# Row maxima of an attention kernel: turned on VectorE by 32x32 blocks instead of on TensorE, with four transfers per half

## The chip, the cores and the metric

The kernel runs on one core of a Trainium2 chip. The metric is the device time of one execution in microseconds (us), the median of several executions. PE is TensorE's matmul, PEld its weight load, DVE is VectorE, ACT is ScalarE, POOL is GpSimd, SP is SyncE, which here only issues transfers.

## What is computed

```python
def proj(W):                                   # x: 8 x 512 x 1024 (batch, channel, token)
    y = jnp.einsum('oc,bct->bto', W, x)
    return y.reshape(B, T, H, Dh).transpose(0, 2, 1, 3)      # 16 heads of 32
Q, K, V = (proj(Wq), proj(Wk), proj(Wv))
att = jnp.einsum('bhqd,bhkd->bhqk', Q, K) * (1.0 / math.sqrt(Dh)) + b[0]
att = att * m + (1.0 - m) * NEG_INF            # m: mask over the keys
att = jax.nn.softmax(att, axis=-1)
y = jnp.einsum('bhqk,bhkd->bhqd', att, V).transpose(0, 2, 1, 3).reshape(B, T, C).transpose(0, 2, 1)
# then, for every row y[b, c, :] of 1024:
q, in_scale = per_token_quant_int8(y)          # absmax / 127, round, clip
out = x + float16(einsum('bsk,nk->bsn', q, weight) * in_scale * w_scale + bias)
```

## The kernel before, in words

The kernel has two parts. `project` computes Q, K and V of all 8 batches, splits Q and K each into a high and a low float32r part and writes them to memory (0 to about 555 us of the span). `attend` runs 32 **steps**; step s is four heads of one batch (`STEPS = B * G`), and all the rest of this section is about it.

**A step has 64 slots** (`UNITS`), t = 0 to 63: two halves of the queries (512 each), times 8 tiles of 128 keys, times 4 heads. In slot t TensorE makes one score tile of 128 keys x 512 queries (L798, in one of three PSUM banks) and ScalarE takes its exponential into `probs` (L932). Since keys lie on the partitions, the row maximum that softmax subtracts can't be a bias of that exponential. It is put into the product instead: `q_stack` has, below the rows of Q, two rows (`ROW_MAX`, partitions 98 and 99) with the high and the low part of minus the row maximum of every query, and `k_stack` has ones there.

**The row maxima are made one step ahead.** In slot t TensorE also makes one tile of 128 queries x 512 keys (L147, `row_max`) into a ring of four PSUM banks, and VectorE reduces it (L154, `reduce_max`). 64 such tiles belong to a step, two for each of 32 pairs (head, tile of queries). The pairs are in two chunks of 16, one per half of the queries. Slots 20 to 63 of step s and slots 0 to 19 of step s+1 make the maxima of step s+1. Chunk 0 of step s+1 is complete at slot 51 of step s, and its rows are needed by slot 0 of step s+1. Chunk 1 of step s is complete at slot 19 of step s and needed by slot 32 (L794: `pe.wait_ge(max_rows[half], ...)`).

**From maxima to rows**, for each chunk: VectorE joins the two halves of a pair, twice over, into 128 x 32 (`join_max`, L161, at slots 19 and 51). TensorE transposes that against an identity into a ring bank (`turn_max`, L169, at slots 20 and 52, `TURN_1` and `TURN_0`). ScalarE takes the high parts (`high_max`, L176) and VectorE the low parts (`low_max`, L182), with a per-partition mark that tells high rows from low rows. SP writes the two rows with one transfer of 32 x 128 elements (`store_max`, L189), whose semaphore `max_rows` TensorE waits for.

**Order of work.** Each engine has its own program, written out by hand slot by slot; only semaphores tie them. What matters here:

- TensorE (`step` of `block.tensor`): in each slot the score, then the row-max tile. After slots 3, 11, 19, 27, 35, 43, 51 and 59 it makes a burst of 16 products probs x V (L829, `weigh`). After slot 27 it also makes the row sums of the step before (L839), after slot 55 eight transposes of the quantised rows (L862), after slot 59 the row sums and the 16 matmuls of the feed-forward product (L872). Each tile that takes a ring bank waits until the bank's last user is done; the list `USES` gives the order, in which each row-max tile, `turn`, `sums` and so on takes the next of the four banks.
- ScalarE: one exponential per slot, and between them copies. Some rows of the next step's `k_stack` and `q_stack` are copies of other rows (`double_k`, L963, two after slot 19 and two after slot 27; `double_q2`, L973, after slots 35 and 59; L968 after slot 59). `take_y` (L937) after slots 3 and 35 empties the bank of the probs x V product. `round_rows` follows slot 43, `make_ints` slot 51. At slot 35 `take_y` comes first, then `double_q2`.
- VectorE: one reduction per slot; `take_absmax` of half 0 and `take_floor` after slot 19 (L1042, L1047), `recip` after slots 27 and 59 (L1028, L1031), `spread` after slots 3 and 31 (L1037), `take_absmax` of half 1 and `scales` after slot 39, `take_qT` at 55.
- GpSimd: additions of whole tiles of exponentials (L1177, `acc`, 128 x 2048, both inputs in SBUF), accumulating transfers (L1161), normalisation (L1184), bias and residual (L1190, L1198), in one fixed order per step. Its transfer for tile pair 2 of half 1 (`begin_pair(s, 1, 2)`) waits for the burst after slot 59, the one for pair 2 of half 0 for the burst after slot 27.
- SP: in each step the transfers of K, of the output, `store_max` for chunk 1, then the loads of Q's second half (`load_q`, L117) and of V, and at the end `store_max` for chunk 0.

Of the kernel before, what the change touches and what calls it, by code (L numbers as in the profile page):

```python
# [25 lines left out]
P = 128  # L26
# [43 lines left out]
EXTRAS = {TURN_1: ("turn",), SUMS_1: ("sums",), TURN_0: ("turn",), TURN_Q: ("turn_q",),  # L70
# [6 lines left out]
MAX_ROWS = 16  # L77
# [80 lines left out]
def join_max(nc, dve, half_max, neg_max, s, chunk, neg_max_done, joined):  # L158

    dve.wait_ge(neg_max_done, HALVES * s + 2 * CHUNK * (chunk + 1))  # L160
    nc.vector.tensor_reduce(neg_max[:, chunk, :].rearrange("p (d c) -> p d c", d=2),  # L161
                            half_max[:, chunk, :, :].rearrange("p (o c) k -> p o c k", o=1).to_broadcast([P, 2, CHUNK, 2]),
                            AX_X, ALU.min).then_inc(joined, 1)


def turn_max(pe, buf, neg_max, ident, s, chunk, joined, maxT_done):

    pe.wait_ge(joined, 2 * s + chunk + 1)
    pe.transpose(buf[0:2 * CHUNK, 0:P], neg_max[:, chunk, :], ident[:, :]).then_inc(maxT_done, 1)  # L169


def high_max(nc, act, buf, max_parts, marks, s, chunk, maxT_done, max_rows, max_hi_done):

    act.wait_ge(maxT_done, 2 * s + chunk + 1)
    wait(act, max_rows[chunk], MAX_ROWS * s)
    nc.scalar.activation(max_parts[:, chunk, :], buf[0:2 * CHUNK, 0:P], ACT.Identity, scale=marks[:, 1:2]).then_inc(max_hi_done, 1)  # L176


def low_max(nc, dve, buf, max_parts, marks, s, chunk, max_hi_done, max_lo_done):

    dve.wait_ge(max_hi_done, 2 * s + chunk + 1)
    nc.vector.scalar_tensor_tensor(max_parts[:, chunk, :], buf[0:2 * CHUNK, 0:P], marks[:, 0:1],  # L182
                                   max_parts[:, chunk, :].bitcast(F32), ALU.mult, ALU.subtract).then_inc(max_lo_done, 1)


def store_max(sp, q_stack, max_parts, par, chunk, max_rows):

    dst = q_stack[par][ROW_MAX:ROW_MAX + 2, chunk, :, :]
    sp.dma_start(dst.bitcast(F32), max_parts[:, chunk, :].bitcast(F32)).then_inc(max_rows[chunk], 16)  # L189


def project(nc, x, mask, wqT, wkT, wvT, qk_d, v_d, bias_d, cond_b, fw, wT, ws_rep, fb_rep, w_scale, f_bias,
# [6 lines left out]
    with ExitStack() as ctx:  # L199
# [54 lines left out]
        def _(sp):  # L254
# [22 lines left out]
            def batch(b, par, last=False):  # L277
# [10 lines left out]
                for tt in range(TT):  # L288
                    if last and tt == TURN_STORE:
                        sp.wait_ge(max_lo_done, 1)  # L290
                        store_max(sp, q_stack, max_parts, 0, 0, max_rows)
# [1011 lines left out]
```

## Time and profile before

| | us |
|---|---|
| median of 3 runs (2295.03 to 2297.74) | 2297.32 |
| the profiled execution, its own time | 2295.35 |
| its span in the trace | 2293.5 |
| PE busy in the span (98%) | 2249.3 |
| POOL busy (74%; 272.4 of the 300 us from 900 to 1200) | 1708.3 |
| DVE busy (70%; 260.4 of the same 300 us) | 1616.1 |
| ACT busy (67%; 243.6 of the same 300 us) | 1538.4 |

The projection fills the first quarter of the span, where VectorE, ScalarE and GpSimd have little to do; the rest is the 32 steps, in which every engine is busy most of the time. Matmul records overlap, so the busy time of PE is not its load: the chain of waits, which gives each piece the time that it adds, is the better view of TensorE. The granted clock of TensorE is 1.00 of full (2.4 GHz) throughout.

### The profile page before, as it was taken

Reading aid. Unit: us, or ns where it says so; the run is one execution under the profiler, and the core shown is the slowest. Engines: PE = TensorE matmul, PEld = TensorE weight load, DVE = VectorE, ACT = ScalarE, POOL = GpSimd, SP = SyncE. Lnnn points to the kernel's source line nnn. Section 1 sums busy time; section 2 is a strip of 40 time slices with the busy share of each in tenths; the row PEclk is TensorE's granted clock in tenths of the full one; section 3 lists DMA queues with packets and bytes.
Section 4 is the critical chain, followed back from the end, with each engine's and each line's share of the span. In section 5 each row is a group of like instructions: output and inputs, shape, how many; then the busy total and the mean of one; then the engine's idle time right before and its main releaser. Section 6 shows DMA issues by size and latency. Waiting matters only on the chain.

```text
span 2293.5 us, 34614 instructions
## 1 busy us (share of the span) xinstructions
PE 2249.3 (98%) x11892; PEld 1354.8 (59%) x11924; DVE 1616.1 (70%) x2779; ACT 1538.4 (67%) x2681; POOL 1708.3 (74%) x735
## 2 busy tenths in 40 slices
PE   9999999999999999999999999999999999999998
PEld 7888888887555555555555555555555555555553
DVE  3311111117888888888888888888888888888883
ACT  3322222223788888887887888888888887888774
POOL 2322333322899998989999998998989989998996
PEclk9999999999999999999999999999999999999999
DMA  6665545575888888888888888888888888888874
GB/s 238 253 229 193 183 183 215 189 219 145 188 186 188 185 185 189 185 191 189 194 187 189 178 189 183 190 187 187 187 184 187 189 188 191 189 189 189 181 155 109
DMA packets 137909, 433.27 MB, mean 189 GB/s; under 512 B 12248, under 2 KB 48088, under 8 KB 113440
## 3 DMA queue, kind: packets, MB, share of 16 engines
q0 software_dynamic: 27360, 199.24, 44.2%
q1 hardware_dynamic: 101040, 205.85, 29.5%
q10 hardware_dynamic: 9360, 26.22, 3.2%
q8 instruction: 91, 1.49, 0.3%
q14 instruction: 58, 0.48, 0.1%
HBM read 130.06 MB, written 100.93 MB: 101 GB/s over the span
## 4 chain that ended last, share of the span: by engine, by line
PE 91%; ACT 3%; POOL 2%; DMA 2%; issue 1%; DVE 0%; POOLq 0%; ACTq 0%
PE score L798 21%; PE pv L829 20%; PE ring L147 19%; PE ring L344 11%; PE score L344 9%; PE ring L872 4%; PE pv L344 3%; PE ring L839 2%; POOL acc L1177 2%; DMA probs<-probs 1%; ACT q_stack L973 1%; ACT probs L932 1%; PE ring L862 1%; ACT y_raw L937 1%; PE ring L169 0%
## 5 line engine op out<-in xcount | busy, mean ns | idle before, releaser
L154 DVE TENSOR_REDUCE half_max<-ring 128x1 f32<-128x512 f32 x2048 | 1261.9, 678 | 92.2 <-PE ring L147 84.4
L932 ACT ACTIVATE probs<-score 128x512 f32<-128x512 f32 x2039 | 1032.6, 615 | 235.0 <-PE score L798 233.5
L1177 POOL TENSOR_TENSOR acc<-acc,probs 128x2048 f32<-128x2048 f32 x189 | 903.6, 4781 | 29.0 <-DMA probs<-probs 26.9
L798 PE MATMUL score<-q_stack,k_stack 100*128 100x512 f32 x2039 | 855.6, 421 | 25.0 <-ACT probs L932 25.0
L147 PE MATMUL ring<-k_stack,q_stack 98*128 98x512 f32 x2048 | 815.1, 398 | 1.7 <-issue 1.7
L798 PEld LDWEIGHTS score<-q_stack,k_stack 100*128 100x128 f32 x2039 | 383.2, 188 | 386.3 <-issue 184.4
L829 PE MATMUL pv<-probs,v_in 128*32 128x512 f32 x4096 | 492.5, 598 | 0.0
L147 PEld LDWEIGHTS ring<-k_stack,q_stack 98*128 98x128 f32 x2048 | 388.4, 190 | 65.0 <-DVE qT L1084 9.0
L1177 POOL TENSOR_TENSOR acc<-probs 128x2048 f32<-128x2048 f32 x63 | 297.8, 4727 | 30.3 <-DMA probs<-probs 15.6
L562 POOL TENSOR_TENSOR q_stack<-x_raw,k_stack 128x1024 fp32r<-128x1024 f32 x28 | 67.8, 2462 | 294.0 <-ACT k_stack L426 294.0
L1161 POOL DMA_DIRECT2D probs<-probs x190 | 192.4, 1012 | 102.8 <-PE pv L829 92.2
L829 PEld LDWEIGHTS pv<-probs,v_in 128*32 128x32 f32 x4096 | 106.9, 109 | 231.8 <-ACT probs L932 143.9
L502 DVE TENSOR_TENSOR part_lo<-score,part_hi 128x512 fp32r<-128x512 f32 x24 | 16.2, 690 | 181.1 <-ACT part_hi L453 181.1
L576 POOL TENSOR_TENSOR part_lo<-k_scaled,part_hi 128x512 fp32r<-128x512 f32 x64 | 82.3, 1304 | 55.3 <-ACT part_hi L456 55.3
L963 ACT ACTIVATE k_stack<-k_stack 32x1024 fp32r<-32x1024 f32 x120 | 120.1, 1047 | 1.5
L456 ACT ACTIVATE part_hi<-k_scaled 128x512 fp32r<-128x512 f32 x64 | 39.3, 629 | 115.9 <-DVE k_scaled L513 87.4
L872 PE MATMUL ring<-fw,qT 128*128 128x512 bf16 x480 | 108.8, 379 | 5.9 <-issue 4.9
L344 PE MATMUL ring<-q_stack,w_hi 128*128 128x512 f32 x256 | 101.3, 396 | 0.0
L344 PE MATMUL ring<-k_stack,w_lo 128*128 128x512 f32 x256 | 101.2, 395 | 0.0
L1184 POOL TENSOR_TENSOR y<-y_raw,factor 128x512 f32<-128x512 f32 x63 | 98.4, 1562 | 2.2 <-DVE factor L1037 2.2
L344 PE MATMUL ring<-k_stack,w_hi 128*128 128x512 f32 x256 | 99.5, 396 | 0.0
L1190 POOL TENSOR_TENSOR half<-prod,fb_rep 128x512 f16<-128x512 f32 x63 | 89.2, 1416 | 12.9 <-DVE prod L1089 12.9
(118 smaller groups left out, 2117.6 us busy)
## 6 DMA issues: line engine op xcount, KB each, us to landing
probs<-probs POOLq DMA_DIRECT2D x190, 1024.0 KB, 8.4
q_stack<-qk_part SPq DMA_DIRECT2D x132, 256.0 KB, 4.3
k_stack<-qk_part SPq DMA_DIRECT2D x66, 512.0 KB
qk_part<-part_hi SPq DMA_DIRECT2D x64, 512.0 KB, 2.7
qk_part<-part_lo SPq DMA_DIRECT2D x64, 512.0 KB, 3.6
v_steps<-v_out SPq DMA_DIRECT2D x64, 256.0 KB, 2.3
v_in<-v_steps SPq DMA_DIRECT2D x32, 512.0 KB, 4.7
v_out<-x ACTq DMA_DIRECT2D x31, 512.0 KB, 8.1
```

The lines of the kernel that those rows point to most:

```text
L147: pe.matmul(bank[:, :], q_stack[par][0:ROW_MAX, chunk, h, qt * P:(qt + 1) * P], k_stack[par][0:ROW_MAX, h, half * N:(half + 1) * N], start ...
L154: nc.vector.tensor_reduce(half_max[:, pair // CHUNK, pair % CHUNK, half:half + 1], bank[:, :], AX_X, ALU.max, negate=True).then_inc(neg_ma ...
L344: return pe.matmul(bank[:, :], lhsT, rhs, start=(k == 0), stop=(k == 3 * CT - 1))
L798: pe.matmul(score[score_bank(s, t)][:, :], k_stack[par][0:ROWS, h, kt * P:(kt + 1) * P], q_stack[par][0:ROWS, half, h, :], start=True, sto ...
L829: mm = pe.matmul(pv[h * DH:(h + 1) * DH, :], v_in[:, par, kt % TT, h * DH:(h + 1) * DH], probs[:, kt % RING, h, :], start=(kt % TT == 0), ...
L872: mm = pe.matmul(buf[:, :], qT[:, tt, :], fw[:, tt, cols], start=(tt == 0), stop=(tt == TT - 1))
L932: nc.scalar.activation(probs[:, kt, h, :], score[score_bank(s, t)][:, :], ACT.Exp).then_inc(exp_done, 1)
L963: nc.scalar.activation(k_stack[s % 2][2 * DH:3 * DH, h, :], k_stack[s % 2][0:DH, h, :].bitcast(F32), ACT.Copy).then_inc(k_doubled, 1)
L1161: pool.dma_start(probs[:, b, :, :], probs[:, a, :, :], accum_op=ALU.add).then_inc(pair_done[i], 16)
L1177: nc.gpsimd.tensor_tensor(acc[:, half, :, :], first, probs[:, tile, :, :], ALU.add).then_inc(acc_done, 1)
L1184: nc.gpsimd.tensor_tensor(y[:, half * N:(half + 1) * N], y_raw[:, half, :], factor[:, half, :], ALU.mult).then_inc(y_done, 1)
L1190: nc.gpsimd.tensor_tensor(half16[:, half, :], prod[:, half, :], fb_rep[:, half * N:(half + 1) * N], ALU.add).then_inc(half_done, 1)
```

## The change

The join, the split into high and low part and the turning of the row maxima are all done by VectorE, in a row, at slots 19 and 51 (`split_max`): a reduction to 128 x 16, a copy to float32r (high part), a subtraction (low part) and a transpose by 32x32 blocks. A block transpose leaves the queries of each 32-partition group in that group, so `store_max` issues four transfers of 32 x 32 elements instead of one. TensorE's transpose, ScalarE's `high_max` and VectorE's `low_max` go; their ring places stay in the list but are unused. Three other items move: on ScalarE three of the four `double_k` now come after slot 27 and one after slot 19, `double_q2` at slot 35 comes ahead of `take_y`; on VectorE `take_absmax` of half 0 and `take_floor` come after slot 27 instead of slot 19.

```diff
-EXTRAS = {TURN_1: ("turn",), SUMS_1: ("sums",), TURN_0: ("turn",), TURN_Q: ("turn_q",),
+EXTRAS = {TURN_1: ("unused",), SUMS_1: ("sums",), TURN_0: ("unused",), TURN_Q: ("turn_q",),
-MAX_ROWS = 16
+MAX_ROWS = 64
...
+def split_max(nc, dve, half_max, neg_max, max_parts, max_turned, s, chunk, neg_max_done, joined, max_hi_done, max_lo_done,
+              max_rows, max_turn_done):
+
+    n = 2 * s + chunk + 1
     dve.wait_ge(neg_max_done, HALVES * s + 2 * CHUNK * (chunk + 1))
...
+    nc.vector.tensor_reduce(neg_max[:, chunk, :], half_max[:, chunk, :, :], AX_X, ALU.min).then_inc(joined, 1)
+    dve.wait_ge(joined, n)
+    nc.vector.tensor_copy(max_parts[:, chunk, 0:CHUNK], neg_max[:, chunk, :]).then_inc(max_hi_done, 1)
+    dve.wait_ge(max_hi_done, n)
+    nc.vector.tensor_tensor(max_parts[:, chunk, CHUNK:2 * CHUNK], neg_max[:, chunk, :], max_parts[:, chunk, 0:CHUNK].bitcast(F32),
+                            ALU.subtract).then_inc(max_lo_done, 1)
+    dve.wait_ge(max_lo_done, n)
+    wait(dve, max_rows[chunk], MAX_ROWS * s)
+    nc.vector.transpose(max_turned[:, chunk, :], max_parts[:, chunk, :].bitcast(F32)).then_inc(max_turn_done, 1)
+
+
+def store_max(sp, q_stack, max_turned, par, chunk, max_rows):
+
+    rows = q_stack[par][ROW_MAX:ROW_MAX + 2, chunk, :, :].rearrange("r h (a g j) -> r h a g j", g=P // DH, j=DH)
+    for g in range(P // DH):
+        sp.dma_start(rows[:, :, :, g, :].bitcast(F32), max_turned[g * DH:(g + 1) * DH, chunk, :]).then_inc(max_rows[chunk], 16)
...
@@ TensorE, step @@
-                    if t == TURN_1:
-                        turn_max(pe, take_ring(s, ("turn", t)), neg_max, ident, s, 1, joined, maxT_done)
...
-                    if t == TURN_0 and ahead:
-                        turn_max(pe, take_ring(s, ("turn", t)), neg_max, ident, s + 1, 0, joined, maxT_done)
...
@@ ScalarE, step @@
                     if prev and ahead and t == 19:
                         double_k(s + 1, 0)
-                        double_k(s + 1, 1)
                     if prev and ahead and t == 27:
-                        double_k(s + 1, 2)
-                        double_k(s + 1, 3)
+                        for h in range(1, GH):
+                            double_k(s + 1, h)
+                    if prev and ahead and t == 35:
+                        double_q2(s + 1, 0)
                     if t == GH - 1 and prev:
                         take_y(s - 1, 1)
-                    if t == TURN_1:
-                        high_max(nc, act, ring_of(("turn", t)), max_parts, marks, s, 1, maxT_done, max_rows, max_hi_done)
                     if t == UNITS // 2 + GH - 1:
                         take_y(s, 0)
-                    if prev and ahead and t == 35:
-                        double_q2(s + 1, 0)
...
-                    if t == TURN_0 and ahead:
-                        high_max(nc, act, ring_of(("turn", t)), max_parts, marks, s + 1, 0, maxT_done, max_rows, max_hi_done)
...
@@ VectorE, step @@
                     if t == OWN - 1:
-                        join_max(nc, dve, half_max, neg_max, s, 1, neg_max_done, joined)
+                        split_max(nc, dve, half_max, neg_max, max_parts, max_turned, s, 1, neg_max_done, joined, max_hi_done,
+                                  max_lo_done, max_rows, max_turn_done)
                     if t == GH - 1 and prev:
                         spread(s - 1, 0)
-                    if t == TURN_1 - 1 and prev:
+                    if t == SUMS_1 and prev:
                         take_absmax(s - 1, 0)
                         take_floor(s - 1)
-                    if t == TURN_1:
-                        low_max(nc, dve, ring_of(("turn", t)), max_parts, marks, s, 1, max_hi_done, max_lo_done)
...
                     if t == OWN + 2 * CHUNK - 1 and ahead:
-                        join_max(nc, dve, half_max, neg_max, s + 1, 0, neg_max_done, joined)
-                    if t == TURN_0 and ahead:
-                        low_max(nc, dve, ring_of(("turn", t)), max_parts, marks, s + 1, 0, max_hi_done, max_lo_done)
+                        split_max(nc, dve, half_max, neg_max, max_parts, max_turned, s + 1, 0, neg_max_done, joined, max_hi_done,
+                                  max_lo_done, max_rows, max_turn_done)
```

The same replacement is made once in the projection, for chunk 0 of step 0 (join, turn, store at its end), and the small tensor `marks` with its three instructions goes.

## Rows read from the trace of the kernel before

**Rows 1.** The page's busy times: busy us (share of the span) xinstructions

```profile
PE 2249.3 (98%) x11892; PEld 1354.8 (59%) x11924; DVE 1616.1 (70%) x2779; ACT 1538.4 (67%) x2681; POOL 1708.3 (74%) x735
```

**Rows 2.** The chain of waits, 1200 to 1260 us: start us, us, what

```profile
1199.59 1.85 PE pv L829 x16
...
1211.19 1.85 PE pv L829 x16
...
1217.44 1.85 PE pv L829 x16
...
1224.12 1.90 PE pv L829 x16
1226.04 0.44 ACT y_raw L937
1226.66 1.06 ACT q_stack L973
1227.74 0.61 ACT probs L932
1228.39 0.50 PE score L798
...
1231.08 1.85 PE pv L829 x16
...
1236.88 1.85 PE pv L829 x16
1238.73 0.43 PE score L798
...
1243.43 1.85 PE pv L829 x16
...
1253.46 1.85 PE pv L829 x16
```

**Rows 3.** The chain of waits around slot 20, same columns

```profile
1213.70 0.11 PE ring L169
```

**Rows 4.** ScalarE's timeline: start us, us, engine line op out<-in xcount [idle before <-releaser]

```profile
1218.10 2.00 ACT L963 ACTIVATE k_stack<-k_stack 32x1024 fp32r<-32x1024 f32 x2
1220.70 4.03 ACT L932 ACTIVATE probs<-score 128x512 f32<-128x512 f32 x8 [0.60 <-PE score L798]
```

**Rows 5.** VectorE's timeline, slots 12 to 20 and slot 52, same columns

```profile
1207.97 4.88 DVE L154 TENSOR_REDUCE half_max<-ring 128x1 f32<-128x512 f32 x8 [0.94 <-PE ring L147]
1212.88 0.22 DVE L161 TENSOR_REDUCE neg_max<-half_max 128x32 f32<-128x64 f32 x1
...
1239.43 0.69 DVE L154 TENSOR_REDUCE half_max<-ring 128x1 f32<-128x512 f32 x1 [0.66 <-PE ring L147]
```

**Rows 6.** Groups of instructions by line, block transposes: xcount | busy us, mean ns | idle

```profile
L1037 DVE STREAM_TRANSPOSE factor<-recips 128x512 f32<-128x512 f32 x64 | 45.0, 703 | 0.1
```

**Rows 7.** Timeline of the span's end, GpSimd and VectorE

```profile
2287.99 1.15 POOL L1198 TENSOR_TENSOR v_out<-v_out,half 128x512 f32<-128x512 f32 x1
2288.33 1.36 DVE L1076 TENSOR_TENSOR half<-prod,fb_rep 128x512 f16<-128x512 f32 x1
...
2289.73 0.69 DVE L1079 TENSOR_TENSOR v_out<-v_out,half 128x512 f32<-128x512 f32 x1
```

**Rows 8.** GpSimd's timeline in the same step

```profile
1210.96 4.88 POOL L1177 TENSOR_TENSOR acc<-acc,probs 128x2048 f32<-128x2048 f32 x1
1216.24 4.58 POOL L1177 TENSOR_TENSOR acc<-probs 128x2048 f32<-128x2048 f32 x1 [0.40 <-DMA probs<-probs]
1220.76 0.88 POOL L1161 DMA_DIRECT2D probs<-probs  x1
...
1236.68 4.58 POOL L1177 TENSOR_TENSOR acc<-acc,probs 128x2048 f32<-128x2048 f32 x1 [0.54 <-DMA probs<-probs]
...
1245.90 0.85 POOL L1161 DMA_DIRECT2D probs<-probs  x1 [3.84 <-PE pv L829]
```

**Rows 9.** SP's transfer of the rows: xcount: duration ns min/median/max, first and last start us

```profile
L189 SPq DMA_DIRECT2D q_stack<-max_parts x64: 622/700/722, 552.0 to 2238.0; - x64
```

**Rows 10.** The page's DMA issues: xcount, KB each, median us to landing

```profile
q_stack<-qk_part SPq DMA_DIRECT2D x132, 256.0 KB, 4.3
```

More of the change, by code:

```diff
@@ L166, in turn_max @@
[L166 to L176, printed above, removed]
@@ L192, in project @@
+def store_max(sp, q_stack, max_turned, par, chunk, max_rows):
+    rows = q_stack[par][ROW_MAX:ROW_MAX + 2, chunk, :, :].rearrange("r h (a g j) -> r h a g j", g=P // DH, j=DH)
+    for g in range(P // DH):
+        sp.dma_start(rows[:, :, :, g, :].bitcast(F32), max_turned[g * DH:(g + 1) * DH, chunk, :]).then_inc(max_rows[chunk], 16)
 def project(nc, x, mask, wqT, wkT, wvT, qk_d, v_d, bias_d, cond_b, fw, wT, ws_rep, fb_rep, w_scale, f_bias,
-            banks, ring, q_stack, k_stack, half_max, neg_max, max_parts, marks, ident, v_out, v_stored,
+            banks, ring, q_stack, k_stack, half_max, neg_max, max_parts, max_turned, ident, v_out, v_stored,
@@ L248, in project @@
         V_BANKS = tuple((bank + SCORES - TT) % SCORES for bank in range(SCORES))
-        TURN_BANK = banks[7]
         TURN_AFTER = CHUNK + 2
@@ L461, in batch @@
                         nc.scalar.activation(v_out[:, i % 2, :], bank[:, :], ACT.Copy).then_inc(v_done, 1)
-                        if last and i == TURN_STORE - 1:
-                            act.wait_ge(marks_set, 3)
-                            high_max(nc, act, TURN_BANK, max_parts, marks, 0, 0, maxT_done, max_rows, max_hi_done)
                     if n == TT - 1 and isinstance(b, int) and b == 0:
@@ L589, in attend @@
 def attend(nc, x, qk_d, v_d, bias_d, fw, ws_rep, fb_rep, out,
-           banks, ring, q_stack, k_stack, half_max, neg_max, max_parts, marks, ident, v_out, v_stored,
+           banks, ring, q_stack, k_stack, half_max, neg_max, max_parts, max_turned, ident, v_out, v_stored,
            stack_set, k_loaded, q1_loaded, q2_loaded, rowmax_done, neg_max_done,
-           ident_set, joined, maxT_done, max_hi_done, max_lo_done, max_rows,
+           ident_set, joined, max_hi_done, max_lo_done, max_turn_done, max_rows,
            block, sems, v_in, v_loaded, proj_done, part_stored, v_done, fw_done):
@@ L704, in step @@
                     store_out(s - 2, 0)
-                sp.wait_ge(max_lo_done, 2 * s + 2)
-                store_max(sp, q_stack, max_parts, par, 1, max_rows)
+                sp.wait_ge(max_turn_done, 2 * s + 2)
+                store_max(sp, q_stack, max_turned, par, 1, max_rows)
                 if ahead:
@@ L719, in step @@
                 if ahead:
-                    sp.wait_ge(max_lo_done, 2 * s + 3)
-                    store_max(sp, q_stack, max_parts, 1 - par, 0, max_rows)
+                    sp.wait_ge(max_turn_done, 2 * s + 3)
+                    store_max(sp, q_stack, max_turned, 1 - par, 0, max_rows)
             sp.wait_ge(proj_done, PROJECTED)
@@ L1273, in program @@
         block = ctx.enter_context(nc.Block())
-        shared = (banks, ring, q_stack, k_stack, half_max, neg_max, max_parts, marks, ident, v_out, v_stored,
+        shared = (banks, ring, q_stack, k_stack, half_max, neg_max, max_parts, max_turned, ident, v_out, v_stored,
                   stack_set, k_loaded, q1_loaded, q2_loaded, rowmax_done, neg_max_done,
-                  ident_set, joined, maxT_done, max_hi_done, max_lo_done, max_rows,
+                  ident_set, joined, max_hi_done, max_lo_done, max_turn_done, max_rows,
                   block, sems, v_in, v_loaded, proj_done, part_stored, v_done, fw_done)
```

49 lines of the change are left out of this document (11 added, 38 removed).

## The prediction

> **What bounds the kernel now.** I read the page's busy times first: PE 98% [rows 1]. That number hides small stalls, because matmul records overlap, so I went to the chain of waits, which lists what each piece adds. Read there the start of each probs x V burst; the steps repeat with a period of 1253.46 - 1199.59 = 53.87 us, and 30 of the 32 are full steps of this kind. The bursts after slots 11 (left out), 19, 27, 35, 43, 51, 59 and the next 3 cut the step into stretches of eight slots [rows 2]:
>
> - slots 4 to 19 (two stretches): 11.60
> - 20 to 27: 6.25
> - 28 to 35, with the row sums: 6.68
> - 36 to 43: 6.96
> - 44 to 51: 5.80
> - 52 to 59, with the eight transposes: 6.55
> - 60 to 3, with row sums and feed-forward: 10.03
>
> The bare stretch is 5.80: a burst of 1.85, a first score of 0.43 and fifteen matmuls at (5.80 - 2.28) / 15 = 0.235 each. TensorE's throughput is the bound nearly everywhere. What it loses is 1.16 us in slots 36 to 43 and 0.45 in slots 20 to 27.
>
> **Where the 1.16 us come from.** At 1226.04 the burst is over, ScalarE takes y (0.44 in the chain), then copies rows of q_stack (L973, 1.06), then makes the exponential that frees the bank for the score at 1228.39 [rows 2]. A score that had to wait costs 0.50 instead of 0.235, as its weight load is no longer hidden [rows 2].
>
> **The change, part by part**, in the clock of the step shown.
>
> *ScalarE's order at slot 35.* The copy goes ahead of take_y. The eight exponentials of slots 28 to 35 begin at 1220.70 and take 4.03, to 1224.73 [rows 4]; y is ready at 1226.04 [rows 2]. The copy's 1.06 fits between. If that cover were gone, the 1.06 would be back. I take 5.85 for slots 36 to 43, with 0.05 for what follows.
>
> *Three double_k after slot 27, one after slot 19.* Two take 2.00 from 1218.10, and ScalarE then idled 0.60 [rows 4]. A third of 1.00 makes it 0.40 late. Three score banks give the exponentials that much room before TensorE waits; the exponentials run at (4.03 - 0.61) / 7 = 0.49 each against TensorE's 0.47 per slot, so over five slots about 0.1 is lost: 6.78 for slots 28 to 35. Bounds: 0 and 0.4.
>
> *TensorE's transpose, high_max, low_max removed.* The transpose adds 0.11 to the chain [rows 3], twice a step. With one double_k fewer, slots 20 to 27 would be bare, 5.80; slots 52 to 59 become 6.55 - 0.11 = 6.44.
>
> *take_absmax and take_floor moved to slot 27.* About 0.8 us, where VectorE waits for the row sums: the last reduction before the sums is over 1.7 us after the burst began (1212.88 - 1211.19 shows the same point in the stretch before [rows 2, 5]), and the burst and sums last 2.7. Nothing.
>
> *VectorE's new burst.* Its own work is small. A reduction of 512 columns takes 0.69 and one of 64 takes 0.22 [rows 5], so a column costs about 0.001 and the fixed part is about 0.15. The reduction of 32 is then 0.19, copy and subtraction of 16 each 0.15 to 0.2 (0.69 for 512 [rows 7]), the transpose of 32 is 0.703 - 0.48 = 0.22 [rows 6]. With gaps of 0.03, 0.8 us. After the last reduction VectorE would stand idle until its next tile: at slot 52 it begins 1239.43 - 1236.88 = 2.55 after the burst [rows 2, 5], while the maxima are ready at 1.7. So, if undisturbed, the burst is hidden: 0.
>
> *What disturbs it: GpSimd.* The subtraction has both inputs in SBUF. In the steps shown VectorE never runs such an instruction; its other work there has at most one tensor in SBUF. The only place beside a busy GpSimd is the end of the span: L1076 and L1079 are both additions of 128 x 512 with two SBUF inputs. L1079 takes 0.69. L1076 began at 2288.33, while GpSimd's L1198 ran until 2289.14, and took 1.36: it ended 0.55 after GpSimd did, which is the streaming of its own 512 columns [rows 7]. It made no progress until GpSimd's instruction was over. At slots 19 and 51 GpSimd is not in a 1.15 us instruction but in a 4.6 to 4.9 us one: 1210.96 to 1215.84 and 1236.68 to 1241.26 [rows 8], while the burst's copy and subtraction would run at about 1213.1 and 1238.8. This is where I choose: I take it that 16 columns wait like 512.
>
> The page "SBUF — State Buffer" of the Trainium skill (section Who interferes with whom) says this as a rule: VectorE's second SBUF input, and both ports in a two-port mode such as an fp32 copy, go through ports shared with GpSimd, held for the whole instruction, whatever its size. By it the sum is the one below. The trace agrees in its one case above. The skill's page "VectorE: DVE Perf Modes" (The three transpose paths) calls VectorE the fastest place for a 32x32 transpose; by that alone the sum would be the first rival's.
>
> *Slot 19.* The subtraction is over soon after 1215.84; with the transpose the next reduction, of slot 20, starts about 0.4 later, at 1216.24, and ends at 1216.93. The ring has four banks and the unused place takes one, so the row-max tile of slot 23 waits for that very reduction. It then costs 0.50: next score at 1217.47. Undelayed that score would start 1.85 + 0.43 + 7 x 0.235 = 3.92 after 1211.19, at 1215.11. Delay 2.36, and the stretch is 5.80 + 2.36 = 8.16. VectorE (0.61 per reduction, 4.88 / 8 [rows 5]) catches up inside the next burst.
>
> *Slot 51.* The burst after slot 27 moves to 1219.35. GpSimd's transfer at 1220.76 needs that burst, and gets it 2.47 after its start (1245.90 - 1243.43 [rows 2, 8]), at 1221.82, so its later work slips 1.06 and the addition ends at 1242.32. The burst after slot 51 begins at 1219.35 + 6.78 + 5.85 + 5.80 = 1237.78. The reduction of slot 52 starts at 1242.72 and ends at 1243.41; the tile of slot 55 waits for it; next score at 1243.95 instead of 1237.78 + 3.92 = 1241.70. Delay 2.25: 6.44 + 2.25 = 8.69.
>
> Both overlaps recur in every step, because GpSimd's order starts anew from its wait for the burst after slot 59 (3.84 us idle [rows 8]), and nothing between that and slot 19 changes.
>
> *SP.* Four issues of 0.70 [rows 9] instead of one: 2.8 us, with the loads of Q behind them. The burst ends near 1216.2, the last issue at 1219.0; with the 4.3 us of a 256 KB load [rows 10] as upper bound for landing, 1223.3. The rows are needed at slot 32, at 1219.35 + 2.71 + 0.2 + 4 x 0.47 = 1224.1. Hidden, with 0.8 to spare; Q's copy is needed at 1227. At slot 51 there are over 6 us more. Ends: nothing, or 1 us per step if an issue costs 1.2. "DMA: Bandwidth & Descriptors" of the Trainium skill (Specifications) says that pieces under 512 B are written less efficiently, and these have 128 B; no row here has such a transfer.
>
> **The sum.** 11.60 + 8.16 + 6.78 + 5.85 + 5.80 + 8.69 + 10.03 = 56.91 us per step, 3.04 more than 53.87; times 30 is 91. Step 0 adds about 2 (slot 51 only; at slot 19 it waits for other things). The last step has no row-max tiles after slot 19 and the projection's tail has an idle GpSimd: nothing. From the profiled execution's 2295.35 that is 2388; the runs' median lies 2 above it: 2390.
>
> **The rivals.**
>
> 1. *The small instructions don't wait for GpSimd.* Then slots 20 to 27 take 5.80 and 52 to 59 6.44: 11.60 + 5.80 + 6.78 + 5.85 + 5.80 + 6.44 + 10.03 = 52.30, 1.57 less, times 30 = 47: 2250. For it: the row that shows the wait is one instruction of 512 columns, and 16 columns might pass between GpSimd's reads. Against: there the second input got nothing at all for 0.7 us. It decides if VectorE is late by less than 0.4 us at slot 23 (3.68 after the burst, against a reduction's end at 3.24). Faster, chance 0.12.
> 2. *Only one of the two bursts meets GpSimd's addition*, by a shift that I misjudged: about 3.04 - 2.3 = 0.7 per step, 2318. Both lie more than 1.7 us inside an addition, so chance 0.05.
> 3. *The subtraction also misses the gap.* At slot 19 the copy waits too, and GpSimd's next addition begins 0.40 after the last one ended [rows 8]. If it comes first, VectorE waits another 4.6: 30 x 4.6 = 138 more, 2528. The copy needs 0.1 of the 0.40: chance 0.05.
> 4. *The four transfers land too late*, 1 us per step on top: 2420. Chance 0.08.
>
> **How the numbers follow.** The forecast has 0.70. Its own range is 2350 to 2420: a delay of 0.3 less or 0.5 more at each of two places. The range to hold 8 in 10 leaves out rivals 1 and 3 and takes in half of rival 2: 2330 to 2430. The chances: slower by over 0.2% (4.6 us, about what a measurement of this kernel can tell from no change) 0.70 + 0.05 + 0.05 + 0.08 = 0.88, less 0.02 for a balance of gain and loss; faster 0.12; within 0.2%, 0.02.
>
> **What would show each step.** Right: in VectorE's timeline the copy or the subtraction at slots 19 and 51 lasts 2 to 3 us instead of 0.2 and ends as L1177 does; TensorE's row-max tile has a new wait for VectorE at slots 23 and 55; bursts 8.2 and 8.7 us apart there, 5.8 after slot 35; L973 no longer in the chain. Wrong: all four new instructions under 0.3 us and a step of 52.3; or the 1.16 us still there; or TensorE waiting for transfers at slot 32.

## The result, and the profile after

| | before | after |
|---|---|---|
| median of 4 runs, us | 2296.79 | 2493.21 |
| the runs, us | 2295.03 to 2297.74 | 2484.2 to 2494.25 |
| ratio after / before | | 1.084 [1.0827, 1.0854] |
| the profiled execution, its span, us | 2295.35, 2293.5 | 2494.25, 2492.4 |
| mean granted TensorE clock | 1.00 | 0.949 |

The kernel became 8.4% slower. I had forecast slower, but 2390 us and at most 2430: 103 us of the 196 were not foreseen. The page's busy times, to be read beside [rows 1], do not show the loss: TensorE seems nearly as busy, VectorE busier by 177 us.

```profile
PE 2353.6 (94%) x11860; PEld 1432.3 (57%) x11860; DVE 1793.2 (72%) x2904; ACT 1541.9 (62%) x2617; POOL 1708.4 (69%) x735
```

The page's chain, by engine:

```profile
PE 70%; DVE 28%; issue 1%; ACT 0%; DMA 0%; ACTq 0%
```

VectorE holds 28% of it. VectorE's groups by line say where (count | busy us, mean ns | idle); the transpose answers to [rows 6]:

```profile
L165 DVE CAST max_parts<-neg_max 128x16 fp32r<-128x16 f32 x64 | 172.8, 2700 | 2.2
L171 DVE STREAM_TRANSPOSE max_turned<-max_parts 128x32 f32<-128x32 f32 x64 | 13.5, 212 | 2.2
L163 DVE TENSOR_REDUCE neg_max<-half_max 128x16 f32<-128x32 f32 x64 | 11.9, 186 | 2.2
L167 DVE TENSOR_TENSOR max_parts<-neg_max,max_parts 128x16 fp32r<-128x16 f32 x64 | 11.2, 175 | 2.2
```

Three of the four new instructions cost what the prediction says (0.19, 0.15 to 0.2, 0.22 us). The copy of 16 columns takes 2.70. VectorE's timeline at slot 19 of one step (start us, us, what), to be read beside [rows 5]:

```profile
1231.08 0.19 DVE L163 TENSOR_REDUCE neg_max<-half_max 128x16 f32<-128x32 f32 x1
1231.30 2.83 DVE L165 CAST max_parts<-neg_max 128x16 fp32r<-128x16 f32 x1
1234.17 0.18 DVE L167 TENSOR_TENSOR max_parts<-neg_max,max_parts 128x16 fp32r<-128x16 f32 x1
1234.38 0.21 DVE L171 STREAM_TRANSPOSE max_turned<-max_parts 128x32 f32<-128x32 f32 x1
...
1259.28 2.68 DVE L165 CAST max_parts<-neg_max 128x16 fp32r<-128x16 f32 x1
```

And GpSimd's at the same time, beside [rows 8]:

```profile
1229.28 4.81 POOL L1135 TENSOR_TENSOR acc<-acc,probs 128x2048 f32<-128x2048 f32 x1
1234.44 4.56 POOL L1135 TENSOR_TENSOR acc<-probs 128x2048 f32<-128x2048 f32 x1 [0.35 <-DMA probs<-probs]
...
1257.36 4.56 POOL L1135 TENSOR_TENSOR acc<-acc,probs 128x2048 f32<-128x2048 f32 x1 [0.39 <-DMA probs<-probs]
```

The copy at 1231.30 ends at 1234.13, GpSimd's addition at 1234.09; the copy at 1259.28 ends at 1261.96, the addition at 1261.92. Of the 64 copies in the trace 62 take over 1 us, and 61 of these end within 0.06 us of the end of an instruction of GpSimd. The subtraction comes in the 0.35 us before GpSimd's next addition and takes 0.18. Now the chain of waits through the same step (start us, us, what), beside [rows 2]:

```profile
1226.17 4.88 DVE half_max L154 x8
1231.30 2.85 DVE max_parts L165
1234.59 0.58 DVE half_max L154
1235.22 0.50 PE ring L147
1235.72 0.40 PE score L767
1236.12 0.43 PE ring L147
1236.54 0.43 PE score L767
...
1239.10 1.85 PE pv L798 x16
...
1244.36 0.24 PE score L767
...
1262.42 0.58 DVE half_max L154
1263.05 0.79 PE ring L147
...
1265.25 0.43 PE ring L147
1265.68 0.43 PE score L767
...
1268.24 2.62 PE pv L798 x16
```

TensorE's row-max tile of slot 23 starts at 1235.22, when the late reduction frees its bank. What follows is the part that I missed: each matmul then adds 0.43 us instead of 0.24 until the burst at 1239.10, and after the second wait the burst itself takes 2.62 instead of 1.85. The windows of these stretches show why (start:end, us, busy of PE, PEld, DVE, ACT, POOL, then granted clock, DMA share, GB/s):

```profile
1229.00:1234.00 5.00, 4.11 (x25) 1.69 (x23) 4.93 (x6) 4.16 (x8) 5.00 (x2) 1.00 0.89 184
1234.00:1239.00 5.00, 3.78 (x9) 2.54 (x9) 4.77 (x10) 2.08 (x4) 4.65 (x2) 0.66 0.05 11
1239.00:1246.00 7.00, 7.00 (x45) 3.76 (x48) 5.52 (x11) 6.89 (x12) 4.42 (x3) 1.00 0.97 238
1263.00:1269.00 6.00, 5.95 (x21) 3.79 (x25) 5.21 (x8) 2.92 (x5) 0.00 (x0) 0.50 0.92 191
```

A granted clock of 0.50 is 1.2 GHz; the 0.66 is a stretch of both levels. TensorE idled 2.11 us before the tile at 1235.22. Stretches of eight slots, from burst to burst as in the prediction, medians over the 30 full steps in us ("e" are experiments below; the prediction's 11.60 for slots 4 to 19 stands halved):

| slots | before | predicted | after | e5 | e1 | e3 |
|---|---|---|---|---|---|---|
| 4-11, 12-19 | 5.80 | 5.80 | 5.8 | 5.8 | 5.8 | 5.8 |
| 20-27 | 6.24 | 8.16 | **9.70** | 8.23 | 5.8 | 5.96 |
| 28-35 | 6.67 | 6.78 | 6.89 | 6.89 | 6.97 | 6.98 |
| 36-43 | 6.97 | 5.85 | 5.79 | 5.81 | 5.8 | 5.8 |
| 44-51 | 5.80 | 5.80 | 5.81 | 5.8 | 5.91 | 6.4 |
| 52-59 | 6.55 | 8.69 | **9.92** | 8.41 | 6.31 | 6.56 |
| 60-3 | 10.03 | 10.03 | 10.29 | 10.02 | 10.02 | 10.03 |
| all 30 steps | 1615.5 | 1707 | 1809.7 | 1712.8 | 1624.1 | 1619.7 |

### The profile page after: what moved, and what is told of

Same layout as the page of the kernel before. It is cut to its first block, busy times and chain, and to the rows that moved or that the text cites. A ratio compares the mean times of both kernels' runs of the same rounds, so it can differ in the third digit from the quotient of the medians.

```text
span 2492.4 us, 34705 instructions
## 1 busy us (share of the span) xinstructions
PE 2353.6 (94%) x11860; PEld 1432.3 (57%) x11860; DVE 1793.2 (72%) x2904; ACT 1541.9 (62%) x2617; POOL 1708.4 (69%) x735
## 4 chain that ended last, share of the span: by engine, by line
PE 70%; DVE 28%; issue 1%; ACT 0%; DMA 0%; ACTq 0%
DVE half_max L154 19%; PE ring L147 14%; PE score L767 13%; PE pv L798 13%; PE ring L331 10%; PE score L331 9%; DVE max_parts L165 7%; PE ring L841 5%; PE pv L331 3%; PE ring L808 2%; PE ring L831 1%; DVE absmax L1002 1%; DVE max_turned L171 1%; DVE neg_max L163 0%; DVE max_parts L167 0%
## 5 line engine op out<-in xcount | busy, mean ns | idle before, releaser
L897 ACT ACTIVATE probs<-score 128x512 f32<-128x512 f32 x2039 | 1049.6, 622 | 466.3 <-PE score L767 464.8
L147 PE MATMUL ring<-k_stack,q_stack 98*128 98x512 f32 x2048 | 870.1, 425 | 127.6 <-DVE half_max L154 126.2
L767 PE MATMUL score<-q_stack,k_stack 100*128 100x512 f32 x2039 | 886.0, 436 | 0.3 <-ACT probs L897 0.3
L767 PEld LDWEIGHTS score<-q_stack,k_stack 100*128 100x128 f32 x2039 | 409.4, 201 | 318.8 <-issue 187.0
L147 PEld LDWEIGHTS ring<-k_stack,q_stack 98*128 98x128 f32 x2048 | 417.8, 204 | 218.7 <-DVE half_max L154 152.7
L798 PE MATMUL pv<-probs,v_in 128*32 128x512 f32 x4096 | 514.4, 621 | 0.0
L165 DVE CAST max_parts<-neg_max 128x16 fp32r<-128x16 f32 x64 | 172.8, 2700 | 2.2
L988 DVE STREAM_TRANSPOSE sums_turned<-ring 128x512 f32<-128x512 f32 x64 | 45.9, 717 | 117.9 <-PE ring L808 117.7
L841 PE MATMUL ring<-fw,qT 128*128 128x512 bf16 x512 | 116.1, 380 | 0.8 <-DVE qT L1044 0.8
```

Of the source, the lines that this page charges most:

```text
L147: pe.matmul(bank[:, :], q_stack[par][0:ROW_MAX, chunk, h, qt * P:(qt + 1) * P], k_stack[par][0:ROW_MAX, h, half * N:(half + 1) * N], start ...
L165: nc.vector.tensor_copy(max_parts[:, chunk, 0:CHUNK], neg_max[:, chunk, :]).then_inc(max_hi_done, 1)
L767: pe.matmul(score[score_bank(s, t)][:, :], k_stack[par][0:ROWS, h, kt * P:(kt + 1) * P], q_stack[par][0:ROWS, half, h, :], start=True, sto ...
L798: mm = pe.matmul(pv[h * DH:(h + 1) * DH, :], v_in[:, par, kt % TT, h * DH:(h + 1) * DH], probs[:, kt % RING, h, :], start=(kt % TT == 0), ...
L841: mm = pe.matmul(buf[:, :], qT[:, tt, :], fw[:, tt, cols], start=(tt == 0), stop=(tt == TT - 1))
L897: nc.scalar.activation(probs[:, kt, h, :], score[score_bank(s, t)][:, :], ACT.Exp).then_inc(exp_done, 1)
```

## The experiments

The kernel before, run beside them on the same chip, took 2295.78 to 2299.94 us in the median of each batch. The times of e2, e4, e5, e6, e12, e14 and e15 are of one run each and have no interval.

### Which instruction waits for GpSimd

**e2_no_copy**: the kernel after; the high part comes from a second reduction, the subtraction stays.

```diff
+    nc.vector.tensor_reduce(max_parts[:, chunk, 0:CHUNK], half_max[:, chunk, :, :], AX_X, ALU.min).then_inc(max_hi_done, 1)
-    nc.vector.tensor_copy(max_parts[:, chunk, 0:CHUNK], neg_max[:, chunk, :]).then_inc(max_hi_done, 1)
```

> The changed kernel with the copy gone: the high part is a second reduction straight from half_max, written as float32r; the subtraction of 128 x 16 with two SBUF inputs stays. In the changed kernel the copy took all of the wait and the subtraction after it never over 0.18 us. Theory (each of the two would wait by itself, the first to come takes the wait): the subtraction now takes 2.3 to 3 us, granted clock near 0.95, 2470 to 2500 us, as the changed kernel. Rival (only the copy waits; a subtraction with two SBUF inputs of 16 columns passes): 0.18 us and 2290 to 2310.

Measured 2472.46 us, clock 0.949. VectorE's groups:

```profile
L167 DVE TENSOR_TENSOR max_parts<-neg_max,max_parts 128x16 fp32r<-128x16 f32 x64 | 161.6, 2526 | 7.0 <-DVE max_parts L164 0.5
```

The wait went over to the subtraction: 2.53 us instead of 0.18.

**e4_copy_alone**: the kernel before with one thing added, an unused copy of 16 columns after each join. **e15_copy_one_column**: the same with one column.

```diff
+    nc.vector.tensor_copy(spare[:, chunk, :], half_max[:, chunk, :, 0])       # e4
+    nc.vector.tensor_copy(spare[:, chunk, 0:1], half_max[:, chunk, 0:1, 0])   # e15
```

> The kernel before with one instruction added after each join: a copy of 128 x 16 in SBUF, float32 to float32r, into a tensor that nobody reads. It waits for no semaphore. Theory (such a copy waits until GpSimd's addition ends, whatever its size): the copy takes 2.3 to 3.5 us instead of 0.18, TensorE stalls at slots 23 and 55, the granted clock falls to about 0.95, 2480 to 2560 us. Rival (the loss needs the chain of four instructions or the four transfers): the copy takes 0.2 us and the time stays at 2297 to 2310.

> The kernel of e4_copy_alone (before, with a spare copy after each join) with one column copied instead of 16. In e4 the copy took 2.34 us in the mean. Theory (any copy in SBUF waits, whatever its size): the same 2 us or more, 2430 to 2460 us. Rival (a single column is copied in the plain way and doesn't meet GpSimd, as the 128 x 1 maximum of take_floor, 0.15 us beside GpSimd's additions in the kernel before, suggests): 0.15 us, 2294 to 2304. I hold the rival for the likelier.

Measured 2449.0 us (clock 0.973) and 2297.16 us (clock 0.998). The copy's group in e4:

```profile
L168 DVE CAST spare<-half_max 128x16 fp32r<-128x16 f32 x63 | 147.6, 2343 | 0.0
```

and in e15:

```profile
L168 DVE CAST spare<-half_max 128x1 fp32r<-128x1 f32 x63 | 9.1, 144 | 0.0
```

One copy of 16 columns that nobody uses makes the kernel before 153 us slower; one column costs nothing. e4 stayed under what was expected, because at slot 51 GpSimd's addition is nearly over when the copy comes: the copy takes 2.94 us in the mean at slot 19 and 1.73 at slot 51. VectorE's timeline in e4:

```profile
1213.16 2.95 DVE L168 CAST spare<-half_max 128x16 fp32r<-128x16 f32 x1
...
1242.69 1.36 DVE L168 CAST spare<-half_max 128x16 fp32r<-128x16 f32 x1
```

There slots 20 to 27 take 9.79 us, but slots 52 to 59 only 7.25. So the copy waits and the subtraction waits, whichever comes first, and either takes the whole of the wait. The Trainium skill's rule that the prediction cites ("SBUF — State Buffer", Who interferes with whom) agrees with e2 and e4. Of one column "VectorE: DVE Perf Modes" (Mode 2×_2P) says that the two-port mode splits the data along its outermost dimension other than 1, which must be even, or equal in source and destination; a single column has no such dimension. e15's 144 ns fit that, but no run shows which mode an instruction took.

### What the clock costs

**e5_filler**: the kernel after, and ahead of the row-max tiles of slots 23 and 55, while TensorE would wait for VectorE, nine matmuls into the unused bank.

```diff
+FILL = {TURN_1 + 3: TURN_1, TURN_0 + 3: TURN_0}
...
+                    if t in FILL and has_max(t, ahead):
+                        own, pair = max_of_slot(s, t)
+                        stack = 1 - par if t >= OWN else par
+                        spot = take_ring(s, ("unused", FILL[t]))
+                        for i in range(9):
+                            row_max(pe, spot, q_stack, k_stack, stack, pair, t % 2, None)
...
```

> The changed kernel, with nine matmuls whose results nobody uses put ahead of the row-max tile of slots 23 and 55, where TensorE waits for VectorE; they go to the unused place's ring bank and take 9 x 0.235 = 2.1 us, a little less than the stall of 2.36 and 2.25 that I worked out. Copy and subtraction stay as they are. Theory (the stalls are as long as worked out, and the rest of the loss is TensorE's clock at half speed after them): the copies still take 2.3 to 3 us, the granted clock is 1.00, the step 57 us, 2390 to 2405. Rival (the stalls are longer for another reason, and the clock costs little): the clock rises but the time stays at 2470 or more.

Measured 2398.52 us, clock 0.996. More work on the engine that bounds the kernel, and 95 us less time. The window from 900 to 1200 us of the kernel after:

```profile
900.00:1200.00 300.00, 282.44 (x1478) 155.65 (x1475) 258.84 (x426) 219.49 (x374) 243.17 (x99) 0.92 0.75 165
```

and of e5:

```profile
900.00:1200.00 300.00, 299.50 (x1654) 170.55 (x1650) 274.39 (x454) 228.88 (x397) 260.60 (x108) 1.00 0.78 175
```

The copy still takes 2.70 us in the mean. With the clock at full level, slots 20 to 27 take 8.23 and 52 to 59 take 8.41 us: the waits alone, close to the prediction's 8.16 and 8.69. The rest of the kernel after, 95 us, is the lower clock behind them. In the 30 steps the stretches 20 to 27, 28 to 35, 52 to 59 and 60 to 3 have 34, 6, 48 and 10 us of it (284.0, 213.3, 306.5 and 310.2 us in the kernel after, 250.0, 207.4, 258.6 and 300.6 in e5).

**e6_slot51_reductions**: the kernel after, with the reductions of e1 (next part) in place of copy and subtraction at slot 51 only; slot 19 still waits.

```diff
+    if chunk == 0:
+        ...
+    else:
```

> The changed kernel with the reductions in place of copy and subtraction at slot 51 alone; slot 19 keeps copy and subtraction. Theory (each of the two waits costs its own stall and its own clock): slots 52 to 59 fall from 9.9 us to about 6.4, slots 20 to 27 stay near 9.7, the granted clock is between 0.95 and 0.99, 2493 - 30 x 3.5 = 2388, 2370 to 2405 us. Rival (the two waits share one loss of clock, or the step is held by something else): under 2350 or over 2430.

Measured 2335.71 us, clock 0.984. Taking away the wait of slot 51 brought slots 52 to 59 to 6.32 us, and the median of slots 20 to 27, where nothing was changed, from 9.70 to 8.2. The median hides that the steps differ. In e6 17 of the 30 steps take 8.5 us or less there and 13 take 8.98 to 10.9; in the kernel after 22 take 9.38 or more, and in e5 only 3 take over 8.3. The sums over the 30 steps are 261.3, 284.0 and 250.0 us. So the wait of slot 19 alone still costs clock in part of the steps, about 11 us against e5, where it cost 34 beside the other wait: the two cannot be priced apart. In e4 slots 20 to 27 lost clock in nearly every step (294.8 us) although its wait at slot 51 was short. What decides whether the clock falls at such a wait, these runs do not show.

### Without the wait: is the first rival's 2250 there?

**e1_reductions**: the kernel after, its copy and subtraction replaced by reductions, which read one tensor: the minimum, minus the rounded minimum, the rounded minimum, and the sum of the first two as low part.

```diff
-    nc.vector.tensor_reduce(neg_max[:, chunk, :], half_max[:, chunk, :, :], AX_X, ALU.min).then_inc(joined, 1)
-    nc.vector.tensor_copy(...)
-    nc.vector.tensor_tensor(...)
+    nc.vector.tensor_reduce(neg_max[:, chunk, :, 0], half_max[:, chunk, :, :], AX_X, ALU.min).then_inc(joined, 1)
+    nc.vector.tensor_reduce(neg_max[:, chunk, :, 1].bitcast(F32R), half_max[:, chunk, :, :], AX_X, ALU.min, negate=True).then_inc(joined, 1)
+    nc.vector.tensor_reduce(max_parts[:, chunk, 0:CHUNK], half_max[:, chunk, :, :], AX_X, ALU.min).then_inc(max_hi_done, 1)
...
+    nc.vector.tensor_reduce(max_parts[:, chunk, CHUNK:2 * CHUNK], neg_max[:, chunk, :, :], AX_X, ALU.add).then_inc(max_lo_done, 1)
```

> The changed kernel, with copy and subtraction replaced by reductions, which have one SBUF input each: high part, its negative and the maximum all straight from half_max, the low part as a reduction over the pair (maximum, minus high part). The block transpose, the four transfers and all moves stay. Theory (the copy's wait for GpSimd's addition, and TensorE's clock that falls after the stall, are the whole loss): no instruction of the burst over 0.25 us, granted clock 1.00, a step of 52.3 us, 2250 us (2240 to 2262). Rival A (four transfers or the longer burst cost something by themselves): clock 1.00, a step over 52.8, 2265 to 2300, with a wait of TensorE for the transfers or for VectorE at slots 23 and 55. Rival B (any small VectorE instruction on SBUF waits there): 2450 or more.

**e3_moves**: the kernel before with the change's three moved items alone (double_k, double_q2, take_absmax with take_floor); TensorE still turns the maxima.

> The kernel before with the three moves alone (one double_k after slot 19 and three after 27, double_q2 ahead of take_y at slot 35, take_absmax and take_floor after slot 27); TensorE still turns the maxima. Theory: slots 36 to 43 from 6.96 to about 5.80, slots 20 to 27 from 6.25 to about 5.9, slots 28 to 35 from 6.68 to at most 6.8, together 1.4 us less per step, 2255 us (2250 to 2265). Rival (what TensorE no longer waits for comes back as a wait for GpSimd or for VectorE later in the step): 2280 or more.

e1: 2297.14 us, ratio to before 1.000 [0.9977, 1.0023] (10 runs). e3: 2305.18 us, ratio 1.0035 [1.0018, 1.0052] (6 runs). All instructions of e1's burst last 176 to 212 ns, and its best step takes 52.24 us (52.67 in e3), as the first rival says (52.30). But single steps are far longer. In e3 slots 44 to 51 take up to 10.75. The chain of waits in such a place, e3:

```profile
1012.30 1.57 POOL y L1183
...
1013.89 0.70 DVE absmax L1041
...
1014.62 0.23 DVE scale L1052
...
1014.86 0.16 DVE inv_scale L1054
```

ScalarE's timeline there:

```profile
1015.06 1.24 ACT L944 ACTIVATE y<-y,magic,inv_scale 128x1024 f32<-128x1024 f32 x1 [3.04 <-DVE inv_scale L1054]
```

and e3's waits over the whole span (who, for whom: us, times, longest):

```profile
POOL acc L1176 <- DMA probs<-probs: 102.1, 69, 3.2
DVE absmax L1041 <- POOL y L1183: 45.3, 22, 8.4
ACT y L944 <- DVE inv_scale L1054: 40.1, 19, 7.5
```

In the kernel before the same three are 42.5 us, 8.9 (twice) and 8.4 (twice). GpSimd is late with y, so VectorE is late with its maximum and the scale, and ScalarE, whose rounding comes in order before the next exponential, stands still. Some clock is lost with it: the mean granted clock is 0.991 in e1 and 0.993 in e3, against 0.999 before.

### What takes the gain back

**e12_moves_light**: e3 with GpSimd's residual addition cut to 32 of 512 columns; it leaves out the addition in the other columns, so its output is incomplete. **e14_reductions_light**: the same in e1.

```diff
-                nc.gpsimd.tensor_tensor(res[:, cols], res[:, cols], half16[:, half, :], ALU.add).then_inc(res_done, 1)
+                few = slice(half * N, half * N + 32)
+                nc.gpsimd.tensor_tensor(res[:, few], res[:, few], half16[:, half, 0:32], ALU.add).then_inc(res_done, 1)
```

> The kernel with the three moves alone, and GpSimd's addition of the residual done on 32 columns instead of 512, so that the output of the other columns is x alone: GpSimd has 2.2 us less work per step, its transfers and its order are the same. Theory (GpSimd's lateness is the whole difference between the 2263 us that the seven other stretches give and the 2305 measured): slots 44 to 51 take 5.8 us in nearly all steps, granted clock 1.00, 2258 to 2268 us. Rival (another wait in those slots): 2290 or more.

> The kernel of e1_reductions with GpSimd's addition of the residual on 32 columns instead of 512 (the output of the other columns is x alone). With GpSimd's lateness out of the way, what the four transfers cost is left. Theory (late landings of the four transfers are a loss of their own): slots 44 to 51 near 5.8, and a sum of slots 60 to 3 that is 5 to 35 us over 30 x 10.03, with waits of TensorE for the row transfers; 2252 to 2280 us. Rival (they come only with GpSimd's lateness): no wait for the row transfers, 2246 to 2252.

e12: 2266.29 us; slots 44 to 51 are back to 176.3 us in all 30 steps (211.7 in e3). So GpSimd is the second bound: with 1.8 us less of its work per step (the residual additions of the run are busy for 33.3 us instead of 91.1) the moves are worth 30 us. e14: 2277.0 us; slots 44 to 51 are as good (176.5), but slots 60 to 3 take 340.5 us in all, against 300.8 in e3, and most of the excess lies in four of the 30 steps (17.3 to 20.0 us instead of 10.0). The four transfers are a loss of their own, seen already in e1's chain of waits (SPq is SyncE's issue):

```profile
1116.14 0.63 SPq L179
...
1116.83 1.19 SPq L179
...
1118.07 1.23 SPq L179
...
1119.33 15.39 DMA q_stack<-max_turned
...
1134.76 0.79 PE score L768
```

**e9_four_alone**: the kernel before with its one row transfer cut in four.

```diff
-MAX_ROWS = 16
+MAX_ROWS = 64
...
-    dst = q_stack[par][ROW_MAX:ROW_MAX + 2, chunk, :, :]
-    sp.dma_start(dst.bitcast(F32), max_parts[:, chunk, :].bitcast(F32)).then_inc(max_rows[chunk], 16)
+    rows = q_stack[par][ROW_MAX:ROW_MAX + 2, chunk, :, :].rearrange("r h (a g j) -> r h a g j", g=P // DH, j=DH)
+    for g in range(P // DH):
+        sp.dma_start(rows[:, :, :, g, :].bitcast(F32), max_parts[:, chunk, g * DH:(g + 1) * DH].bitcast(F32)).then_inc(max_rows[chunk], 16)
```

> The kernel before with the one transfer of 32 x 128 elements cut into four of 32 x 32, nothing else. Theory (at the rhythm of the kernel before four transfers land in time): four issues of 0.7 to 1.1 us, no wait of TensorE for them, 2294 to 2301 us. Rival (the late landings of e1_reductions belong to the four transfers themselves): waits of TensorE for the row transfers and 2310 or more.

Measured 2312.73 us, ratio 1.0079 [1.0062, 1.0096] (4 runs). Its waits from 600 to 2200 us have two lines that the kernel before does not have:

```profile
PEld score L799 <- DMA q_stack<-max_parts: 10.4, 13, 3.0
...
PE score L799 <- DMA q_stack<-max_parts: 5.0, 6, 2.5
```

In the profiled run, the fastest of the four (2304.84 us), slots 60 to 3 take 310.2 us instead of 300.9. Cutting the transfer costs 0.8% by itself. One of the four issues takes no longer than the single one before:

```profile
L190 SPq DMA_DIRECT2D q_stack<-max_parts x256: 610/632/1465, 550.4 to 2250.5; - x128
```

(duration of an issue in ns, min/median/max; [rows 9] has 700 for the single one). "DMA: Bandwidth & Descriptors" of the Trainium skill (Why small descriptors are slow) says that transfers from SBUF to SBUF don't suffer the penalty of small pieces. It speaks of the bandwidth of a large transfer, not of when a small one lands, and no run here changes the size of the pieces without their number. What is measured is that four transfers of 4 KB, with pieces of 128 bytes, land late in some steps: 15.4 us after the start of the last issue in the rows of e1 above. Why, no run here shows.

**e7_moves_loads, e8_reductions_loads**: e3 and e1 with SyncE's loads of Q's second half and of V ahead of the rows of chunk 1, to part these loads from GpSimd's accumulating transfers.

> The kernel with the three moves alone, and in SP's order the loads of Q's second half and of V put ahead of the write of the row maxima of chunk 1, so that they start some 10 us earlier in the step. In e3_moves GpSimd's additions waited 98 us in total for its own accumulating transfers, against 42 in the kernel before, and slots 44 to 51 took up to 10.8 us instead of 5.8. Theory (a shorter step makes GpSimd later against TensorE; its transfer at slot 19 then runs beside SP's loads of Q and V and takes 10 us instead of 7, and it never catches up): GpSimd's waits for its transfers fall under 60 us, slots 44 to 51 are 5.8 in nearly all steps, a step of 52.8 us, 2262 us (2258 to 2275). Rival (GpSimd's own work is too long for a step under 53.5 us, whatever the loads do): 2290 or more.

> The kernel of e1_reductions with the same earlier loads of Q and V. In e1_reductions the four transfers took four issues of up to 1.3 us and landed as late as 15 us after, which TensorE waited for in about ten steps (48 us in all), and GpSimd was late in about fifteen. Theory (both come from transfers that meet in the second third of the step): slots 44 to 51 near 5.8, fewer waits of TensorE for the row transfers, 2250 to 2275 us. Rival (the four transfers land late by themselves, as GpSimd's megabyte is in front of them): the waits for the transfers stay near 40 us, 2280 or more.

2320.84 us, ratio 1.0106 [1.0089, 1.0123], and 2306.36, ratio 1.0051 [1.0034, 1.0068]: both worse than without it. In e7 GpSimd waits 113.9 us for its transfers from 600 to 2200 us (98.2 in e3). So my idea that these loads make GpSimd's transfers land late fell. For the four row transfers e8 shows something else. In e1 TensorE waited for them like this:

```profile
PEld score L768 <- DMA q_stack<-max_turned: 27.5, 10, 7.2
```

and in e8, in its profiled run:

```profile
PEld score L768 <- DMA q_stack<-max_turned: 2.9, 1, 2.9
```

Slots 60 to 3 fell from 329.7 to 302.0 us, while slots 44 to 51 rose from 196.7 to 228.4, and VectorE's wait for y from 33.4 to 65.0. So when the four land depends on what SyncE does around them, and the earlier loads gave more away at GpSimd than they won. Whether it is the order of the transfers or the later rhythm of the step that helped the rows, one pair of traces does not tell.

**e10_moves_gap**: e3, and on GpSimd the bias addition moves ahead of the first addition of the step, so that it fills the wait for a transfer. **e11_reductions_gap**: the same in e1. **e13_moves_gap_both**: the residual addition moves too.

```diff
+                if second:
+                    add_bias(s - 2, 1)
                 add(s, 0, 0)
...
-                if second:
-                    add_bias(s - 2, 1)
```

> The kernel with the three moves alone, and in GpSimd's order the bias addition of the second half (1.3 us) put ahead of add(s, 0, 0), where GpSimd waits for its first accumulating transfer, instead of after normalise(s - 1, 1). Theory (GpSimd, its own transfers in its order, is what a step under 53 us meets): part of the wait is filled with work, normalise comes about 1 us earlier, slots 44 to 51 lose less than the 38 us that they lost in e3_moves, 2262 to 2290 us. Rival (GpSimd's sum of work and transfers counts, not its order): 2300 or more.

> The kernel of e1_reductions with the same change of GpSimd's order. Theory: slots 44 to 51 lose less than the 23 us of e1_reductions; what TensorE waits for the four transfers in slots 60 to 3 (29 us there) stays or not, so 2262 to 2295 us. Rival: 2297 or more.

> As e10_moves_gap, with both the bias and the residual addition of the second half (2.5 us) ahead of add(s, 0, 0). Theory (what GpSimd does while it waits for the transfer is free, up to 3.2 us): as good as e10_moves_gap or better, 2260 to 2285 us. Rival (where the wait is short, the addition comes 2 us later and normalise with it): worse than e10_moves_gap by 5 us or more.

| | us (runs) | ratio to before | slots 44-51, 30 steps | slots 60-3 |
|---|---|---|---|---|
| e10 | 2287.68 (10) | 0.9958 [0.9945, 0.9971] | 198.8 | 300.8 |
| e11 | 2312.95 (6) | 1.0076 [1.0052, 1.0099] | 188.6 | 338.3 |
| e13 | 2301.02 (10) | 1.002 [1.001, 1.0031] | 207.4 | 300.8 |

e10 is the only complete kernel that beats the kernel before, by 0.4% (e12 and e14 leave work out). Its waits, beside those of e3:

```profile
POOL acc L1176 <- DMA probs<-probs: 67.7, 58, 3.0
DVE absmax L1041 <- POOL y L1183: 32.1, 19, 8.1
ACT y L944 <- DVE inv_scale L1054: 27.8, 16, 7.5
```

In e11 slots 44 to 51 gain as well, but slots 60 to 3 lose more to late rows, up to 19.2 us in one step. The best version found thus leaves the turning on TensorE with one transfer, and keeps only the moves and the earlier bias addition.

## Why the prediction was right and wrong

- **The small instructions wait for GpSimd: right.** The price came from one 512-column instruction at the span's end [rows 7]; 16 columns wait like 512 (2.70 us). It is the copy that waits; the subtraction passes in the gap. The row in the prediction was of an instruction with two inputs in SBUF; that a copy waits too, the prediction had from the Trainium skill's page alone, and e4 shows it. Rival 3, with a second wait of 4.6, did not come: the subtraction never took over 0.18.
- **The size of the two waits: right.** 8.16 and 8.69 predicted, 8.23 and 8.41 in e5. The sum by these is 2390; e5 took 2398.5.
- **The failed step is the sum's "Slot 19" and "Slot 51": "Delay 2.36" and "Delay 2.25" were added, and every matmul after them still cost 0.235.** They cost 0.43 until the clock was back. All rows that I read had a granted clock of 1.00, so none could show what a wait of 2 us does; I gave that unknown no bound. It measured 95 us (2493.21 less 2398.52), and the range ended at 2430, 63 below the median. "TensorE: Matmul & The Clock Gate" of the Trainium skill (Part 1) puts the penalty of the warm-up ramp at under 1% of a typical kernel's span. That is a cost paid at the start, and no measure for waits that come back in every step: here those cost 3.8%.
- **Step 36 to 43: right** (5.79 for 5.85). **Three double_k: too small**, 6.89 for 6.78, inside its bound of 0.4.
- **"Hidden" for the four transfers: right for this kernel, not in general.** With the two waits in the step TensorE waits 0.6 us for them in the whole run; slots 60 to 3 take 10.29 for 10.03, but 10.02 in e5, which has the four transfers too, so that is clock. Without the waits it shows: slots 60 to 3 take 40 us more than before in e14 and 29 in e1, and e9, at the pace of the kernel before, is 17 us slower (2312.73 against 2295.78).
- **Rival 1, "2250 without the wait": wrong price.** e1 took 2297. Against the rival's 52.30 a step, e1 has 23 us more in slots 44 to 51 (196.7 less 174), 29 more in slots 60 to 3 (329.7 less 300.9) and 6 more in 28 to 35. I had shortened TensorE's step by 1.57 and left GpSimd as it was, though the table of times shows it busy for 272.4 of 300 us.

## What to carry to other kernels

Before moving small work to VectorE, look at what GpSimd runs at that very moment: here a copy or a subtraction of 16 columns with its inputs in SBUF cost the rest of GpSimd's instruction, while a copy of one column and reductions, even four of them, cost at most 0.21 us each. When a wait of about 2 us, as here, falls on TensorE in every step, price the matmuls that follow at half the clock too, as one end of the range, and test with filler matmuls whether that is the loss. And when the bound engine's step becomes shorter, redo the sum for the next engine and for every transfer that was only just in time.

## What the runs showed of the hardware that was not expected

- A copy of 128x16 float32 in SBUF took 2.34 to 2.70 us on average (at most 4.29) beside GpSimd's additions; the same copy of one column took 0.144.
- After an idle of 2.11 us TensorE's matmuls came 0.43 us apart instead of 0.235, at a granted clock of 0.50, until the next burst. Nine extra matmuls in the idle time gave 95 us back. With one of the two waits gone (e6), slots 20 to 27, behind the other, took 8.98 us or more in 13 of 30 steps instead of 22.
- Of four row transfers in place of one, the last landed 15.4 us after its issue began in one step of e1, where the next score needed it. In e8, with SyncE's loads ahead of the rows of chunk 1, TensorE hardly waited for them.
- Open: why the four land so late, and why GpSimd's own transfers are waited for longer in the shorter step (102.1 us in e3, 42.5 before).
